# A fused Mamba and expert block: another order in the start-up and in the lists of a chunk's items

## What is computed

```python
mod = (silu(c) @ wmod).reshape(4, 6, 1, -1)          # sa, ca, ga, sb, cb, gb; ga and gb kept at least 0.25 from 0
h = layernorm(x) * (1 + ca) + sa
xs, res = split(h @ in_proj_w.T, 2)                  # 512 channels each
xs = silu(conv4(xs) + conv_b)                        # causal, per channel
dt, B, C = split(xs @ x_proj_w.T, [64, 80])          # B, C: 16 states
delta = softplus(dt @ dt_proj_w.T + dt_proj_b)
s_t = exp(delta * A) * s_{t-1} + (delta * xs) * B;  y_t = sum over states of s_t * C_t
x = x + ga * ((y * silu(res)) @ out_proj_w.T)
h = layernorm(x) * (1 + cb) + sb
x = x + gb * (one shared expert + the best of 7 routed experts)(h)
```

## Time and profile before

| | us |
|---|---|
| median of 3 runs (2614.96 to 2616.28) | 2615.27 |
| the profiled execution | 2615.41 |
| its span, first to last instruction | 2613.6 |
| VectorE busy | 1945.9 (74%) |
| GpSimd busy | 1935.3 (74%) |
| TensorE busy | 2209.2 (85%) |
| ScalarE busy | 1387.3 (53%) |

### The profile page before, as it was taken

One profiled execution on the slowest core, in us unless ns is written; L12 is line 12 of the kernel. 1 busy time (PEld: TensorE's weight loads), 2 busy tenths in 40 slices (PEclk: granted clock), 3 DMA queues, 4 the chain that ended last, 5 costly groups with the idle time before them and its releaser, 6 DMA issues. The chain is left out here.

```text
span 2613.6 us, 31166 instructions
## 1 busy us (share of the span) xinstructions
PE 2209.2 (85%) x7664; PEld 1048.8 (40%) x7665; DVE 1945.9 (74%) x2068; ACT 1387.3 (53%) x2474; POOL 1935.3 (74%) x830
## 2 busy tenths in 40 slices
PE   7768898989889897979888989898875758999997
PEld 3223333433434343434333334333332434665664
DVE  2799999898988998989898988899899262222222
ACT  3566666666575756565666666665745222222221
POOL 0689888898988898889888888989899104555553
PEclk9779989898989898989898898989887779999999
DMA  3533342424232323333333424242321052222221
...
DMA packets 149400, 224.39 MB, mean 86 GB/s; under 512 B 48227, under 2 KB 85617, under 8 KB 145138
## 3 DMA queue, kind: packets, MB, share of 16 engines
...
## 5 line engine op out<-in xcount | busy, mean ns | idle before, releaser
L1004 POOL TENSOR_TENSOR hs<-hs,c_rep 128x2048 f32<-128x2048 f32 x256 | 1156.3, 4531 | 150.8 <-ACT state L738 150.6
L839 DVE TENSOR_TENSOR_SCAN hs<-dA,state,hs 128x512 f32<-128x512 f32 x768 | 931.5, 1264 | 61.4 <-ACT dA L731 56.9
L731 ACT ACTIVATE dA<-d_rep,a 128x512 f32<-128x512 f32 x1024 | 684.3, 683 | 315.0 <-DVE hs L839 309.8
L997 POOL TENSOR_TENSOR hs<-u_rep,b_rep 128x2048 f32<-128x2048 f32 x96 | 434.6, 4527 | 52.6 <-DMA u_rep<-us 49.0
L826 DVE TENSOR_TENSOR hs<-u_ps,b_rep 128x2048 f32<-128x2048 f32 x160 | 361.6, 2277 | 10.3 <-issue 5.3
L507 PE MATMUL bank<-hs,spread 128*32 128x512 f32 x2048 | 314.3, 770 | 52.7 <-POOL hs L1004 50.8
L839 DVE TENSOR_TENSOR_SCAN hs<-dA,hs 128x512 f32<-128x512 f32 x256 | 295.0, 1204 | 31.7 <-ACT dA L731 30.0
L436 PE MATMUL bank<-xin,w_in 128*128 128x512 f32 x512 | 267.3, 660 | 59.6 <-ACT xdbl L603 48.2
L478 PE MATMUL bank<-n,w1s 128*128 128x512 f32 x512 | 255.5, 628 | 44.6 <-DVE xpad L862 31.4
L1378 DVE TENSOR_TENSOR hid<-z,sg 128x512 f32<-128x512 f32 x70 | 48.4, 692 | 297.0 <-ACT sg L1356 297.0
L1296 PE MATMUL z<-w1r,hT 128*128 x560 | 260.0, 607 | 3.0 <-issue 1.7
...
...
## 6 DMA issues: line engine op xcount, KB each, us to landing
d_rep<-delta SPq DMA_DIRECT2D x1024, 64.0 KB, 2.0
...
```

The lines of the kernel that those rows point to most:

```text
L731: nc.scalar.activation(dA[:, u % ABANK, :], d_rep[:, q, :], ACT.Exp, scale=t["a"][:, u:u + 1]).then_inc(da_ready, 1)
L839: nc.vector.tensor_tensor_scan(hs[:, s % RING, g, :], dA[:, u % ABANK, :], hs[:, s % RING, g, :], state[:, u:u + 1] if m else 0.0, ALU.mul ...
L997: nc.gpsimd.tensor_tensor(hs[:, s % RING], u_rep[:, i % UBUF, :].unsqueeze(1).to_broadcast([P, NG, T]), b_rep[:, par, :].rearrange("p (g t ...
L1004: nc.gpsimd.tensor_tensor(hs[:, s % RING, :, :], hs[:, s % RING, :, :], c_rep[:, par, :].rearrange("p (g t) -> p g t", g=NG), ALU.mult).th ...
```

## The change

In the start-up: XP and the DT and DB groups stand ahead of all RS groups in `START`, the rows product moves ahead of XP and four column products behind it. SyncE stores B and C as soon as XP is copied, ahead of the stores of the gates; B is loaded before the gates and C after them, each with a semaphore of its own, and the spreads D and U follow without waiting for the scaled weights. GpSimd does the eight weight products and issues the two stores itself, w2 before its first IN and w_out after; the loads of the scaled weights stand behind X of chunk 0. x of chunk 1 goes early into `n2`, which is free then; its layer norm comes early on VectorE, and ScalarE's normalization, the T and the first XS groups come after the fourth decay row of chunk 0. The SiLU of res of chunk 0 joins that of u of chunk 1.

In every chunk: all four lists and `transfers` have a new order. Which of the two shared banks an item gets follows from it.

```diff
         plan = {
-            0: [(('Y', 1), -2), (('XS', 0), 1), (('XS', 1), 1), (('DB', 2), 0)],
-            1: [(('XS', 2), 1), (('DB', 3), 0), (('XS', 3), 1), (('SUM', 3), -1)],
-            2: [(('CV', 0), 1), (('CV', 1), 1), (('OP', 0), -1)],
-            3: [(('CV', 2), 1), (('CV', 3), 1), (('OP', 1), -1)],
+            0: [(('Y', 1), -2), (('XS', 0), 1), (('XS', 1), 1), (('DB', 2), 0), (('XS', 2), 1), (('DB', 3), 0), (('XS', 3), 1)],
+            1: [],
+            2: [(('SUM', 3), -1)],
+            3: [(('CV', 0), 1), (('CV', 1), 1)],
             4: [],
-            5: [(('SUM', 0), 0), (('RS', 0), 1), (('RS', 1), 1)],
-            6: [(('XP', 0), 1), (('RS', 2), 1)],
-            7: [(('RS', 3), 1), (('T2', 0), -1), (('T2', 1), -1)],
-            8: [(('DT', 0), 1), (('DT', 1), 1), (('RB', 0), -1), (('RB', 1), -1)],
-            9: [(('SUM', 1), 0), (('GL', 0), -1), (('B', 0), -1), (('B', 1), -1)],
-            10: [(('DB', 0), 1), (('B', 2), -1), (('B', 3), -1)],
-            11: [(('DT', 2), 1), (('DB', 1), 1), (('DT', 3), 1)],
-            12: [(('A', 0), -1), (('T', 0), 2)],
-            13: [(('SUM', 2), 0)],
-            14: [(('T', 1), 2), (('A', 1), -1), (('A', 2), -1), (('A', 3), -1), (('Y', 0), -1)],
-            15: []}
+            5: [(('OP', 0), -1), (('CV', 2), 1), (('CV', 3), 1), (('OP', 1), -1), (('RS', 0), 1), (('RS', 1), 1), (('SUM', 0), 0), (('XP', 0), 1)],
+            6: [],
+            7: [],
+            8: [(('RS', 2), 1), (('RS', 3), 1), (('T2', 0), -1), (('T2', 1), -1), (('DT', 0), 1), (('DT', 1), 1), (('RB', 0), -1)],
+            9: [(('GL', 0), -1), (('RB', 1), -1), (('SUM', 1), 0), (('B', 0), -1), (('B', 1), -1), (('B', 2), -1), (('DB', 0), 1), (('B', 3), -1), (('DT', 2), 1)],
+            10: [],
+            11: [(('DB', 1), 1), (('DT', 3), 1), (('A', 0), -1)],
+            12: [(('T', 0), 2), (('SUM', 2), 0), (('T', 1), 2)],
+            13: [(('A', 1), -1), (('A', 2), -1)],
+            14: [(('A', 3), -1)],
+            15: [(('Y', 0), -1)]}
         evict = {
-            0: [[], [], [], [(('XS', 0), 1), (('XS', 1), 1)]],
-            1: [[], [(('XS', 2), 1)], [], [(('XS', 3), 1)]],
-            2: [[], [], [(('CV', 0), 1)], []],
-            3: [[], [(('CV', 1), 1)], [], []],
-            4: [[(('CV', 2), 1)], [], [], []],
-            5: [[], [(('CV', 3), 1), (('HALO', 0), 2)], [(('SU', 0), 1)], []],
-            6: [[(('RS', 0), 1), (('RS', 1), 1)], [], [], []],
-            7: [[(('N2', 0), -1)], [], [], []],
-            8: [[(('XP', 0), 1)], [(('RS', 2), 1), (('RS', 3), 1)], [(('T2', 0), -1), (('T2', 1), -1)], [(('DT', 0), 1), (('DT', 1), 1)]],
-            9: [[(('RB', 0), -1)], [], [(('E0', 0), 1)], []],
-            10: [[(('L0', 0), 1), (('RB', 1), -1)], [], [(('B', 0), -1), (('GL', 0), -1)], []],
-            11: [[], [], [(('B', 1), -1)], [(('B', 2), -1)]],
-            12: [[(('B', 3), -1), (('SRS', 0), 0)], [], [], [(('G', 0), -1), (('DT', 2), 1)]],
-            13: [[(('N', 0), 2)], [(('DT', 3), 1)], [], [(('GM0', 0), -1), (('E1', 0), 1)]],
-            14: [[], [], [], []],
-            15: [[(('L1', 0), 1)], [(('GM1', 0), -1), (('T', 0), 2)], [(('T', 1), 2)], []]}
+            0: [[], [], [(('XS', 0), 1)], []],
+            1: [[], [(('XS', 1), 1)], [], [(('XS', 2), 1), (('XS', 3), 1)]],
+            2: [[], [], [], []],
+            3: [[], [], [], [(('CV', 0), 1)]],
+            4: [[], [], [], [(('CV', 1), 1), (('CV', 2), 1)]],
+            5: [[], [], [(('CV', 3), 1)], []],
+            6: [[(('SU', 0), 1)], [], [(('HALO', 0), 2), (('RS', 0), 1)], []],
+            7: [[], [], [(('RS', 1), 1)], [(('XP', 0), 1), (('N2', 0), -1)]],
+            8: [[(('RS', 2), 1)], [(('RS', 3), 1)], [(('T2', 0), -1)], [(('T2', 1), -1)]],
+            9: [[(('DT', 0), 1)], [], [(('DT', 1), 1), (('RB', 0), -1)], []],
+            10: [[(('E0', 0), 1), (('GL', 0), -1), (('L0', 0), 1), (('RB', 1), -1)], [], [(('B', 0), -1)], [(('B', 1), -1)]],
+            11: [[], [], [], [(('B', 2), -1)]],
+            12: [[(('B', 3), -1)], [(('SRS', 0), 0)], [], [(('N', 0), 2), (('G', 0), -1), (('DT', 2), 1), (('DT', 3), 1)]],
+            13: [[], [], [], [(('E1', 0), 1), (('GM0', 0), -1)]],
+            14: [[], [], [], [(('GM1', 0), -1), (('T', 0), 2), (('L1', 0), 1)]],
+            15: [[], [(('T', 1), 2)], [], []]}
         vector = {
             0: [[(('Y', 1), -2)], [], [(('DB', 2), 0)], []],
-            1: [[(('DB', 3), 0)], [], [], []],
-            2: [[], [], [(('SUM', 3), -1)], []],
-            3: [[], [], [], [(('OP', 0), -1)]],
-            4: [[], [], [], [(('OP', 1), -1)]],
-            5: [[], [], [], []],
-            6: [[(('LN2', 0), -1)], [], [(('SUM', 0), 0)], []],
-            7: [[], [], [], []],
+            1: [[], [(('DB', 3), 0)], [], []],
+            2: [[], [], [], []],
+            3: [[(('SUM', 3), -1)], [], [], []],
+            4: [[], [], [], [(('OP', 0), -1)]],
+            5: [[], [], [], [(('OP', 1), -1)]],
+            6: [[(('LN2', 0), -1)], [], [], []],
+            7: [[], [(('SUM', 0), 0)], [], []],
             8: [[], [], [], []],
             9: [[], [], [], []],
-            10: [[(('SUM', 1), 0)], [], [], []],
-            11: [[(('LN', 0), 2)], [(('DB', 0), 1)], [], [(('DB', 1), 1)]],
-            12: [[], [], [], [(('A', 0), -1)]],
-            13: [[], [(('RC', 0), -1)], [], [(('SUM', 2), 0)]],
-            14: [[(('A', 1), -1)], [(('RC', 1), -1)], [(('A', 2), -1)], []],
+            10: [[], [(('SUM', 1), 0), (('LN', 0), 2)], [], []],
+            11: [[], [], [(('DB', 0), 1)], []],
+            12: [[(('DB', 1), 1)], [], [], [(('A', 0), -1), (('RC', 0), -1)]],
+            13: [[], [], [(('SUM', 2), 0)], []],
+            14: [[(('RC', 1), -1), (('A', 1), -1)], [], [(('A', 2), -1)], []],
             15: [[(('A', 3), -1)], [], [], [(('Y', 0), -1)]]}
...
-        transfers = [('U', 5), ('ACC2', 0), ('XR', 0), ('D', 4), ('D', 5), ('W2', 0), ('D', 6), ('U', 7), ('D', 8), ('WO', 0), ('D', 7), ('U', 10),
-                     ('D', 9), ('D', 10), ('D', 11), ('BC', 0), ('U', 13), ('X', 0), ('D', 12), ('ROWS', 0), ('D', 13), ('LOG', 0), ('U', 15), ('D', 14),
-                     ('D', 15), ('D1', 2), ('D1', 0), ('U1', 2), ('D1', 1), ('D1', 3)]
-        FIRST_TRANSFERS = [("D", 0), ("U", 2), ("D", 1), ("D", 2), ("D", 3)]
-        START = [("T", 0), ("T", 1), ("XS", 0), ("XS", 1), ("XS", 2), ("XS", 3), ("CV", 0), ("CV", 1), ("CV", 2), ("CV", 3), ("RS", 0), ("RS", 1), ("XP", 0), ("RS", 2),
-                 ("DT", 0), ("DT", 1), ("RS", 3), ("DT", 2), ("DT", 3), ("DB", 0), ("DB", 1), ("DB", 2), ("DB", 3)]
+        transfers = [('W2', 0), ('ACC2', 0), ('U', 5), ('D', 4), ('XR', 0), ('D', 6), ('U', 7), ('D', 5), ('D', 8), ('U', 10), ('WO', 0), ('D', 7),
+                     ('U', 13), ('D', 10), ('D', 9), ('BC', 0), ('X', 0), ('D', 11), ('ROWS', 0), ('D', 12), ('D', 13), ('D', 15), ('D', 14), ('LOG', 0),
+                     ('U', 15), ('D1', 0), ('U1', 2), ('D1', 2), ('D1', 1), ('D1', 3)]
+        FIRST_TRANSFERS = [("D", 0), ("D", 1), ("D", 2), ("U", 2), ("D", 3)]
+        START = [("T", 0), ("T", 1), ("XS", 0), ("XS", 1), ("XS", 2), ("XS", 3), ("CV", 0), ("CV", 1), ("CV", 2), ("CV", 3), ("XP", 0),
+                 ("DT", 0), ("DT", 1), ("DB", 0), ("DT", 2), ("DT", 3), ("DB", 1), ("RS", 0), ("DB", 2), ("RS", 1), ("DB", 3), ("RS", 2), ("RS", 3)]
...
+            def keep_bc(f):
                 sp.wait_ge(xdbl_ready, f + 1)
                 sp.dma_start(bc_dram, xdbl[DT_ROWS:PROJ, :]).then_inc(bc_kept, 16)
+
+            def load_rep(rep, n, par, loaded):
+                for nf in range(NF):
+                    r = n * STATE + nf * NG
+                    sp.dma_start(rep[DS * nf:DS * nf + DS, par, :],
+                                 bc_dram[r:r + NG, :].rearrange("n t -> (n t)").partition_broadcast(DS)).then_inc(loaded, 16)
+
+            def spread_bc(f, par):
+
+                keep_bc(f)
                 hold(sp, bc_kept, 16 * f + 16, held)
+                if known(f) and f == 1:
+                    sp.wait_ge(scaled, 2 * BATCH)
                 if not known(f) or f >= 2:
                     sp.wait_ge(dbu_own, N_OWN * (f - 1))
                     sp.wait_ge(dbu_shared, N_SHARED * (f - 1))
+                load_rep(b_rep, 0, par, b_loaded)
+                if not known(f) or f >= 2:
                     sp.wait_ge(hc_ready, NSET * (f - 1))
-                for n, rep in enumerate((b_rep, c_rep)):
-                    for nf in range(NF):
-                        r = n * STATE + nf * NG
-                        sp.dma_start(rep[DS * nf:DS * nf + DS, par, :],
-                                     bc_dram[r:r + NG, :].rearrange("n t -> (n t)").partition_broadcast(DS)).then_inc(bc_loaded, 16)
+                load_rep(c_rep, 1, par, crep_loaded)
 
...
+                    if known(c) and c == 0 and kind == "X":
+                        sp.wait_ge(ga_stored, 16)
+                        load_w_out(0)
```

(64 more changed lines are left out.)

89 lines of the change are left out of this document (42 added, 47 removed).

## The result

| | us |
|---|---|
| changed kernel, median of 4 runs (2511.84 to 2514.26) | 2512.46 |
| before, beside it, median of 4 runs (2614.96 to 2616.44) | 2615.78 |
| ratio, with its 95% interval | 0.9606 (0.959 to 0.9623) |
| span of the profiled execution | 2510.4 |

What follows compares the result with a forecast made beforehand. VectorE was taken as nearest the bound, with 11.6 us a chunk without work. 14 chunks by 5.2 (73), start 8, chunk 0 3, last chunk 2, drain 0: 2,615 - 86 = 2,529 us; 8-in-10 range 2,480 to 2,606.

Steps and rivals of the forecast that it cites:

- Only the start gains: Rival, chance 0.15: in the chunks the stalls reappear at other items, so only 11 us go, 2,604 us.
- Slower: Rival, chance 0.10: SUM1 behind GL and RB1 at half rate holds VectorE; with 2 us a chunk lost, 2,632 us.
- 8 + 3: Start-up 8 us (bounds 3 and 15), plus 3 us in chunk 0 (bounds 0 and 5).
- The chain of the second input: Chunk 0 after scan 0: dA row, halo, normalize, XS0 and its copy; scan 4 near 83.6 instead of 91.53.
- The three of chunk 0: Chunk 0: 3 us from shrinking VectorE's 5.51 us wait at 128.77 for the SiLU of u and two RS copies.
- SUM1 made at 67.5, wanted at 68.9: Steady chunk, us from first scan: SUM1 behind GL and RB1 is ready 1.4 us early, removing 2.0 us of dA wait.
- My sign of being wrong: Steady chunk: a SUM wait of over 3 us in every chunk would show the prediction wrong.
- The sign of one stretch at clock 0.5 instead of two: Steady chunk, TensorE's clock: only one half-rate stretch a chunk would be left, where there were two.
- the SUM1 term: Steady chunk: small waits between DT and RB may slow SUM1, giving back 0 to 2.6 us; 1.3 taken.
- full gain: Rival, chance 0.14: TensorE's queue stays dense and at 2.4 GHz, 8 to 8.7 us a chunk, 2,484 down to 2,475 us.
- the same chain in another order: Drain after the last chunk: the same chain of items reordered, gain 0.
- the shared port: Start-up: two-input VectorE instructions and GpSimd ones shut each other out; GpSimd's delay is covered, so the sum stays.

Runs made afterwards that it cites:

- lists_only: Kernel before, with its old start-up, given the changed kernel's four lists and `transfers`: 2517.33 us, ratio 0.962.
- no_gap: Changed kernel with ScalarE's copies of T2 1, DT0, DT1, GL and RB1 earlier in its list, TensorE's list unchanged: 2480.74 us, ratio 0.9478.
- start_only: Changed kernel with the four lists and `transfers` of before, so only the new start-up stays: 2607.22 us, ratio 0.9965.
- adds_early: no_gap with VectorE's DB0 one scan earlier and DB1 one scan and one product earlier: 2488.53 us, ratio 0.9512.

## Why the prediction was right, and where its terms were off

**The bound and the mechanism held.** The lists brought most of the time, as waits of VectorE with one named item each. *Only the start gains* would have been 2,604: *lists_only* alone excludes it. *Slower* needed a chunk to lose on balance; its mechanism, SUM1 behind GL and RB1 at half rate, is there, but cost 2.7 us, and the rest of the gain is larger.

**Start-up and chunk 0**, forecast 8 + 3, measured 10.9. First scan forecast 70.6, came at 69.94; by its own terms the forecast was 71.4 (67 and twice 2.2), and the spreads were there 1.5 us sooner (65.53). The fifth was forecast at 83.6 and came at 82.82; the B/C store, forecast near 47, came at 46.58. That DB2 and DB3 stand behind RS0 and RS1 in `START`, and not ahead of all RS groups as said, changes no sum. The chain of the second input was priced rightly. The three of chunk 0 were near in size (2.2), for a partly wrong reason: the 5.51 us wait only shrank to 4.50, and *lists_only* gains 6.1 us up to chunk 1 without the new start, so that the two parts overlap there, which the sum had left out.

**The chunk**, forecast 5.2, measured 6.1. (122.7 less 5.2 is a period of 117.5, not 117.7.) Forecast as removed were 8.7 us: DB, OP, A, and the dA waits behind CV0 and B; 7.7 went. Forecast as coming back were 3.5, 2.2 for SUM2 and 1.3 for SUM1; 2.2 came, but the other way round. SUM2 is late in six of fourteen chunks only, 0.6 us on the mean, and SUM1 in every chunk, 2.8 on the mean; of these 3.4 us, 1.2 stood at the SUMs before as well. Two terms were off in opposite directions, and that they partly cancel is luck. The step that was mis-sized is "SUM1 made at 67.5, wanted at 68.9": with the first scan at 772.0 it was made at 72.6 and wanted at 70.0, since I let TensorE run from DT to RB without idle and at full rate, and then took half the possible loss (1.3). My sign of being wrong, a SUM wait of over 3 us in every chunk, was nearly there: it is over 3 us in four chunks and 2.4 or more in all. The sign of one stretch at clock 0.5 instead of two failed: there are still two (830 to 842 and 858 to 862). *no_gap* shows what the SUM1 term was worth: without that wait a chunk takes 115.1 us, 8.2 under before. Its total lies in the range of my rival *full gain*, but not by that rival's mechanism: TensorE's queue isn't dense or at 2.4 GHz throughout, and 8 us of it are the drain's. The change missed this by ScalarE's order around T2, GL and RB1.

**The drain**, forecast 0, measured 8.0: the largest error after the chunks' 12. I said "the same chain in another order" and did not read its rows: three A groups and a B group at 3.8 us each stood in the trace of before, where they take 2.0 in a chunk. *lists_only* and *start_only* put these 8 us down to the lists. Why TensorE's clock is granted again for A2 after and not before (in both, A1 follows 3.00 us of idle and A2 one of 0.78) these runs don't settle.

**Chunk 15**, forecast 2, measured 0.1; I had given it a part of a steady chunk's gain. In the trace its dA waits fall from 4.1 to 1.7 us and its wait of 0.9 for A goes, but it waits 1.58 us for SUM1 and 2.65 for SUM2, where before it waited 1.15 for SUMs. SUM2 is late there because it stands 8.45 us for GpSimd's product (8.83 before).

**The two rules.** On the shared port (Trainium skill, SBUF — State Buffer, "SBUF: two separate sides"), which I had left out of the sum: here a clash does show. VectorE's product of delta and u took 1.22 us before GpSimd had begun and 1.99 while it worked, and GpSimd's four took 10.25 us beside it and 9.25 without. A lock that the one holds while the other waits fits both numbers, and as said there it does not change the sum. No experiment isolated it. On the clock (Trainium skill, TensorE: Matmul & The Clock Gate, "Why this matters for your kernels") the trace agrees that half rate follows an idle stretch. What density is worth is another matter: in *no_gap* a SUM1 of 6.17 us ends no wait of VectorE, and *adds_early*, which cost 7.8 us, brought none of the 1 to 2 us a chunk that its rival expected. In these runs density paid only where it took time off a wait of the bounding engine.
